# Smaller first loads in another order, and a last norm in five units, in a decoder layer on one core

## The reference, cut to what matters

```python
x = _layernorm(x + _L0_ffn_ref(x, gate_w, w1, w2, w3), axis=-1)
```

## Time and profile before

| | us |
|---|---|
| time, median of 3 runs | 710.21 |
| the three runs | 709.97, 710.21, 711.47 |
| the profiled execution, its own time | 709.6 |
| span of the profiled execution | 708.2 |
| busy in it: TensorE, VectorE, ScalarE, GpSimd | 619.1, 403.2, 236.3, 282.1 |
| mean granted TensorE clock in it | 0.925 |

### The profile page before, as it was taken

How to read it: one execution, slowest core, us unless ns; L and a number is a source line. 1 busy time by engine, 2 the same in 40 slices (tenths; PEclk the granted TensorE clock), 3 DMA queues, 4 the chain that set the end, 5 groups by cost and what they waited for, 6 DMA issues and landing times.

```text
span 708.2 us, 13714 instructions
## 1 busy us (share of the span) xinstructions
PE 619.1 (87%) x3843; PEld 495.4 (70%) x3844; DVE 403.2 (57%) x1207; ACT 236.3 (33%) x467; POOL 282.1 (40%) x195
## 2 busy tenths in 40 slices
PE   5999999798698975486999999999999999999940
PEld 2655659586366654365888888888888888888830
DVE  2566488865748769864545545545445455445524
ACT  3544550002776451223223242241422422322204
POOL 7000010011354446667513838348382274751112
PEclk9999999999899787566999999999999999999975
DMA  8999308104000033222511161512516115111116
GB/s 291 313 335 337 105 1 216 25 1 178 1 1 2 30 128 150 104 100 61 198 30 28 30 208 30 195 30 50 185 30 208 25 22 205 30 30 31 28 23 233
DMA packets 53429, 74.81 MB, mean 106 GB/s; under 512 B 13328, under 2 KB 49552, under 8 KB 52112
## 3 DMA queue, kind: packets, MB, share of 16 engines
q1 hardware_dynamic: 41056, 60.18, 25.6%
q0 software_dynamic: 6864, 9.11, 7.4%
q10 hardware_dynamic: 5472, 5.06, 2.7%
HBM read 42.67 MB, written 31.67 MB: 105 GB/s over the span
## 4 chain that ended last, share of the span: by engine, by line
PE 68%; DVE 15%; POOL 5%; ACT 5%; issue 3%; DMA 3%; POOLq 0%; ACTq 0%; DVEq 0%; SPq 0%
PE bank L2146 27%; PE bank L2166 12%; PE bank L1727 7%; PE bank L1877 4%; PE bank L2156 4%; POOL experts_w L796 3%; PE bank L1737 2%; DVE region L1230 2%; DVE region L1228 1%; DVE small L1247 1%; PE bank L2026 1%; PE bank L2132 1%; ACT region L1103 1%; PE bank L1982 1%; PE bank L2045 1%
## 5 line engine op out<-in xcount | busy, mean ns | idle before, releaser
L2146 PE MATMUL bank<-experts_w,experts_x 128*128 x864 | 218.7, 402 | 3.6 <-POOL experts_w L796 2.3
L2146 PEld LDWEIGHTS bank<-experts_w,experts_x 128*128 128x128 f32 x864 | 158.7, 190 | 37.6 <-issue 4.5
L1659 DVE TENSOR_TENSOR region<-region,bank 128x512 f32<-128x512 f32 x72 | 49.5, 688 | 165.0 <-ACT region L1054 165.0
L1054 ACT ACTIVATE region<-bank 128x512 f32<-128x512 f32 x72 | 43.0, 597 | 244.7 <-PE bank L2146 244.7
L809 POOL DMA_INDIRECT total<-region,rid x36 | 55.7, 1548 | 171.5 <-DVE region L1673 123.9
L2166 PE MATMUL bank<-experts_w 128*128 x864 | 121.1, 290 | 2.1 <-DVE experts_w L1663 2.1
L2166 PEld LDWEIGHTS bank<-experts_w 128*128 128x128 f32 x864 | 107.9, 191 | 2.5 <-issue 2.3
L796 POOL TENSOR_TENSOR experts_w<-wstage,experts_w 128x3072 f32 x12 | 83.4, 6948 | 0.5
L677 POOL TENSOR_TENSOR small<-small 128x4 f32<-128x4 f32 (+4 forms) x18 | 24.6, 1371 | 106.3 <-DVE small L1239 85.6
L1727 PE MATMUL bank<-xcol,region 128*128 128x512 f32 x128 | 57.9, 610 | 8.9 <-DMA xcol<-in_xT 7.3
L1126 DVE SCALAR_TENSOR_TENSOR region<-bank,convw,region 128x511 f32<-128x511 f32 (+2 forms) x48 | 35.9, 749 | 39.1 <-ACT region L852 37.2
(11 more groups left out here) (333 smaller groups left out, 894.3 us busy)
## 6 DMA issues: line engine op xcount, KB each, us to landing
wstage<-in_w_exp SPq DMA_DIRECT2D x8, 3072.0 KB, 10.7
slots<-padrow SPq DMA_DIRECT2D x8, 2210.0 KB, 19.8
region<-slots ACTq DMA_DIRECT2D x38, 130.0 KB, 2.1
xcol<-in_xT SPq DMA_DIRECT2D x4, 512.0 KB, 7.3
xtok<-in_x SPq DMA_DIRECT2D x1, 2048.0 KB, 12.8
region<-in_ctxT SPq DMA_DIRECT2D x1, 2048.0 KB, 7.9
region<-in_ctx SPq DMA_DIRECT2D x4, 512.0 KB, 9.0
region<-total SPq DMA_DIRECT2D x4, 512.0 KB, 5.5
```

Source lines behind the costliest of these rows:

```text
L1054: act.activation(gsil[:, u], bank[2 * u][:, :], ACT.Silu).then_inc(sil_done, 1)
L1659: dve.tensor_tensor(hmid[:, u], gsil[:, u], bank[2 * u + 1][:, :], ALU.mult).then_inc(mid_done, 1)
L2146: mm = pe.matmul(bank[2 * u + m][:, :], (xTh, xTl)[a][:, s, k, :], moving(off, w, m * KD * F + k * F + u * HALF, HALF), start=(k == 0 and ...
```

## The change

The start: `W_in` comes in four pieces, the first 128 columns of `x_proj` ahead of xT of batch 0; the taps and the bias follow with a semaphore of their own (`ld_taps`), then the first 128 columns of `z`, then the rest of either half, then `wxT`, then xT of batches 1 to 3. TensorE waits for the pieces one by one, ScalarE and VectorE for `ld_taps` in place of `ld_conv`.

The end: the four units of four tiles become five, of 2, 4, 4, 4 and 2 tiles, in the loads, the statistics, the power, the shift, the normalization and the writes.

```diff
+ENDS = ((0, 2), (2, 4), (6, 4), (10, 4), (14, 2))
...
-            sp.dma_start(winT[:, :, 0:DI], w_in[:, :, 0:DI]).then_inc(ld_win[0], 16)
+
+            def weights_of(n, first, last):
+                sp.dma_start(winT[:, :, first:last], w_in[:, :, first:last]).then_inc(ld_win[n], 16)
+            weights_of(0, 0, P)
             input_of(0)
-            sp.dma_start(winT[:, :, DI:], w_in[:, :, DI:]).then_inc(ld_win[1], 16)
-            input_of(1)
-            sp.dma_start(convw, conv_w.rearrange("(j p) k -> p j k", p=P)).then_inc(ld_conv, 16)
-            sp.dma_start(convb[:, :], conv_b).then_inc(ld_conv, 16)
+            sp.dma_start(convw, conv_w.rearrange("(j p) k -> p j k", p=P)).then_inc(ld_taps, 16)
+            sp.dma_start(convb[:, :], conv_b).then_inc(ld_taps, 16)
+            weights_of(1, DI, DI + P)
+            weights_of(2, P, DI)
+            weights_of(3, DI + P, 2 * DI)
             sp.dma_start(wxT, w_xT.rearrange("(j p) n -> p j n", p=P)).then_inc(ld_conv, 16)
-            for b in range(2, B):
+            for b in range(1, B):
                 input_of(b)
...
-            for b in range(B):
-                rsqrt(NQ, NQ * b)
+            for first, n in ENDS:
+                rsqrt(n, first)
...
-                    act.wait_ge(ld_conv, 16 * 3)
+                    act.wait_ge(ld_taps, 16 * 2)
...
-            for b in range(B):
-                act.wait_ge(shift_done, b + 1)
-                for k in range(NQ):
-                    n, row = NQ * b + k, ya[:, NQ * b + k, :]
-                    ins = act.activation(row, row, ACT.Identity, bias=shift[:, n:n + 1], scale=rsy[:, n:n + 1])
+            for u, (first, n) in enumerate(ENDS):
+                act.wait_ge(shift_done, u + 1)
+                for k in range(first, first + n):
+                    row = ya[:, k, :]
+                    ins = act.activation(row, row, ACT.Identity, bias=shift[:, k:k + 1], scale=rsy[:, k:k + 1])
                 ins.then_inc(fin_done, 1)
...
-            dve.wait_ge(ld_conv, 16 * 3)
+            dve.wait_ge(ld_taps, 16 * 2)
...
-            for b in range(B + 1):
-                if b < B:
-                    dve.wait_ge(y_back[b], 16)
-                    norm_stats(NQ * b, NQ, 1e-5, NQ * b, ya)
-                if b:
-                    n = slice(NQ * (b - 1), NQ * b)
-                    dve.wait_ge(rs_done, asked[0] - (1 if b < B else 0))
+            for u in range(len(ENDS) + 1):
+                if u < len(ENDS):
+                    first, n = ENDS[u]
+                    dve.wait_ge(y_back[u], 16)
+                    norm_stats(first, n, 1e-5, first, ya)
+                if u:
+                    first, n = ENDS[u - 1]
+                    n = slice(first, first + n)
+                    dve.wait_ge(rs_done, asked[0] - (1 if u < len(ENDS) else 0))
...
             for n in range(B * NJ):
                 if n % NJ == 0:
                     pe.wait_ge(ld_xT[n // NJ], 16)
+                if n == 1:
+                    pe.wait_ge(ld_win[2], 16)
                 project("xp", n)
-                if n == 0:
-                    pe.wait_ge(ld_win[1], 16)
+                if n < 2:
+                    pe.wait_ge(ld_win[1 + 2 * n], 16)
```

More of the change, by code:

```diff
@@ L409, in decoder_kernel @@
         drained = [sem(f"bank{k}_drained") for k in range(8)]
-        ld_conv, ld_x, ld_small, ld_ctx = (sem(f"{n}_loaded") for n in ("conv", "x", "small", "ctx"))
-        ld_win, ld_xT = [sem(f"win{n}_loaded") for n in range(2)], [sem(f"xT{b}_loaded") for b in range(B)]
+        ld_taps, ld_conv, ld_x, ld_small, ld_ctx = (sem(f"{n}_loaded") for n in ("taps", "conv", "x", "small", "ctx"))
+        ld_win, ld_xT = [sem(f"win{n}_loaded") for n in range(4)], [sem(f"xT{b}_loaded") for b in range(B)]
         consts_done = sem("consts_done")
@@ L444, in decoder_kernel @@
             "slots_cleared", "first_loaded", "first_silu_done", "first_high_done", "first_sent"))
-        y_back = [sem(f"yback{b}_loaded") for b in range(B)]
+        y_back = [sem(f"yback{n}_loaded") for n in range(len(ENDS))]
         shift_done, fin_done, out_done = sem("shift_done"), sem("fin_done"), sem("out_done")
@@ L539, in _, with rows_of @@
                 sp.wait_ge(y_sent[s], sent)
-            for b in range(B):
-                sp.dma_start(ya[:, b * NQ:(b + 1) * NQ, :], total[b * S:(b + 1) * S, :].rearrange("(i p) d -> p i d", p=P)
-                             ).then_inc(y_back[b], 16)
-            for b in range(B):
[L544 to L547, removed]
+            def rows_of(t, u):
+                first, n = ENDS[u]
+                return t[first * P:(first + n) * P, :].rearrange("(i p) d -> p i d", p=P)
+            for u, (first, n) in enumerate(ENDS):
+                sp.dma_start(ya[:, first:first + n, :], rows_of(total, u)).then_inc(y_back[u], 16)
+            for u, (first, n) in enumerate(ENDS):
+                sp.wait_ge(fin_done, u + 1)
+                sp.dma_start(rows_of(out, u), ya[:, first:first + n, :]).then_inc(out_done, 16)
+            sp.wait_ge(out_done, 16 * len(ENDS))
         def scan_step_by_step(pool):
@@ L1757, in _ @@
                         pe.wait_ge(consts_done, 1)
-                        pe.wait_ge(ld_conv, 16 * 3)
+                        pe.wait_ge(ld_conv, 16)
                     scan_inputs(n // NJ - 1)
```

## The result

The changed kernel took **708.18 us** (median of 17 runs, 703.55 to 709.77), the kernel before 710.26 us (17 runs, 705.75 to 711.52): a ratio of 0.9963 with a 95% interval of 0.9947 to 0.998. The profiled execution of the change took 708.43 us with a span of 707.0, against 709.6 and 708.2.

The account below looks back on a forecast made before the run. The prediction took TensorE's chain to bound the kernel, with waits at the start and ScalarE plus the last write at the end; -1.25 - 0.2 - 0.35 = -1.8 us gave 708.4 against a 710.21 median, range 706.9 to 710.3.

Parts of the forecast that it names:

- xT at 5.9: Start: xT of batch 0 lands at 5.9 instead of 7.16, TensorE starts at 6.05, 1.25 us earlier.
- Rival 1: Start gives nothing: xT needs its 5.56 us regardless of bytes ahead; only the end's 0.55 remains, 709.65; chance 0.14.
- The lower bound of 4.0: Start: 512 KB alone took 4.0 us, so xT, issued at 1.60, lands not before 5.6.
- the 0.4 us that the prediction worked out from the page: Start: at 138 GB/s the first 128 KB takes 0.95 us instead of some 0.55, making the sum -1.4 instead of -1.8.
- No wait for the pieces: Start: TensorE never waits for `W_in` pieces; `z` 0's 128 KB lands near 7.0, needed at 9.6, cover 2.6 us.
- ScalarE 1.25 us earlier, with its table load at 9.7: Start: taps land near 6.5 to 7, so ScalarE and its 1.28 us table load, placed after the wait, start 1.25 earlier.
- TensorE's tie with bank 0: Start: TensorE wanted the bank at 15.60 and had it within the usual 0.24; this tie moves as a whole.
- `scan_inputs` near 28.7: Start: the first `scan_inputs` comes near 28.7 in place of 29.93.
- The end, 0.55 us: After the last expert: ScalarE's end 0.2 us earlier and the smaller last write 0.35 us shorter.
- Rival 4: End gives nothing: unit 1 lands as late as 694.2 and ScalarE's gap eats the write's saving; 709.0; chance 0.12.
- The gain travels through: Between start and end: the stretch is untouched and paced by TensorE, so the start's 1.25 us gain should reach the end.
- rival 3: Clock falls elsewhere: one more half-speed fall gives 710.0 (chance 0.13), one fewer 706.8 (chance 0.08).

Follow-up runs that it names:

- the later one: The change run again beside the kernel before on one chip: 708.69 us (12 runs) against 709.83 (23 runs), ratio 1.0002.
- start alone: The change with its end set back to four units of four tiles, against the kernel before: 707.71 us against 709.68, ratio 0.9975.
- small last unit: The change with end units of 4, 4, 4, 2 and 2 tiles: one run, 704.04 us.
- VectorE last: The change with end units of 2, 4, 4, 2, 4, VectorE normalizing the last; 708.59 us against 710.89 for the kernel before, ratio 0.9973.
- early matmuls: The change plus nine constant matmuls before TensorE's first wait, against the kernel before: 702.82 us, ratio 0.9916; repeated, 706.68 us, ratio 0.9962.
- end alone: The kernel before with only the change's end, its start set back: 708.74 us, ratio 0.9984 against the kernel before.
- the one run with a pause of 2.1 us: The change with the 128 KB of weights for `z` 0 moved behind xT of batch 1 and `wxT`: one run, 713.45 us.
- the pieces alone: `W_in` in four pieces, taps and bias left behind xT of batch 1, end as before: 709.50 us, ratio 1.0006 against the kernel before.
- the taps alone: Taps and bias ahead of the second half of `W_in`, kept in two halves, end as before: 709.50 us, ratio 1.0003 against the kernel before.

## Why the prediction was right

It said 708.4 for the median and 1.8 us of gain; measured were 708.18 and 2.1. That the median came out this near is in part luck. The profiled pair differs by 1.2 us, not 1.8, since 0.6 of the start's gain was lost on the way. And the times of either kernel lie in two groups: in this comparison 6 of the 17 runs of the change are below 707 and 1 of 17 before, in the later one 2 of 12 and 8 of 23, with 1.1 us between the medians. The two local gains do not rest on the median. By its steps, in the profile of the change:

- **xT at 5.9.** It landed at 5.73, 4.13 us after its issue; in the seven profiles with 640 KB up to its end whose chain shows it it took 3.90 to 4.86 us, 4.29 in the mean, which is the forecast 5.9 (the change twice, start alone, small last unit, VectorE last, early matmuls twice). Rival 1 falls. The lower bound of 4.0 was 0.1 too high. The windows show that the smaller pieces moved more slowly: 213 GB/s up to 4.8 us where the earlier trace rows have 236. The landing came all the same 0.2 us before the time taken from bytes, so the small first piece cost nothing that could be seen. (The Trainium skill, "DMA: Bandwidth & Descriptors", section Bandwidth, gives small transfers a lower rate. The trace agrees in direction, but the taps' small pieces lie in the same stretch, and the 0.4 us that the prediction worked out from the page did not appear in the landing.)

```profile
2.00:4.80 2.80, 0.00 (x0) 0.00 (x0) 0.00 (x0) 0.00 (x0) 2.26 (x9) 1.00 0.78 213
```

- **No wait for the pieces.** None: the 128 KB for `z` 0 took 3.3 us from 3.16 and were there at 6.5 (7.0 expected), 3 us before they were needed; the 384 KB pieces at 8.0 and 9.1.
- **ScalarE 1.25 us earlier, with its table load at 9.7.** This step was wrong. The prediction had the table load behind the wait for `xp` 0; it stands behind the wait for the bias and ahead of the other. VectorE gained 2.57 us (13.12 to 10.55), not 1.25. It cost nothing in the sum, since TensorE's tie with bank 0 became a slack, and it is what let the early matmuls work later.
- **`scan_inputs` near 28.7.** 28.79, 28.59 in the second profile. The term that strayed is the number of slow matmuls, which the prediction had fixed at 3.55 us: the 48 took 22.24 to 23.84 us over the profiles without early matmuls in which TensorE met no wait of its own.
- **The end, 0.55 us.** 0.6: ScalarE's start at 6.58 (6.8 expected), gap 1.02 (0.95), end at 15.71 (15.9), last write 2.7 us (2.5). Each was within 0.25. The two terms were off in opposite directions: ScalarE's end gave 0.35 in place of 0.2, the rest up to the end of the span 0.24 in place of 0.35. GpSimd's power of two columns took 0.72 us, not the 1.01 of four. Rival 4 falls: unit 1's statistics began 4.46 us after the issue, not 5.5.
- **The gain travels through.** It did until 136 us. Then one longer stretch of half clock took 1.5, and by the loads of `total` 0.6 was left. So this step was not right as it stands: what lies between is untouched, but the clock in it moved. That is rival 3, which happened inside the very execution that was profiled, beside the forecast and not in place of it; the range, which was to take it in, begins at 706.9, 0.1 above its lower side. With the first matmul at 5.7 to 7.3 us, 3 to 7 gaps behind it were slow, and that moment does not settle how many: at 7.26 (end alone) they were 7, at 7.29 4. The statement in the Trainium skill, "TensorE: Matmul & The Clock Gate", Part 1, that the gate's interval does not start with the kernel, fits this.

The ratio's interval in the first comparison excludes no change, and in the later one it does not. With all runs of both taken together (29 of the change in two comparisons, 92 of before in four), the medians are 708.5 and 709.9, 1.4 us apart, a little under the profiles' own sum of 1.2 + 0.6. Sorted at 707 after the fact, the upper group's medians are 708.7 and 710.1, again 1.4 apart. That a single program spreads over 5 us is shown; that the change's moment of starting makes the quick patterns more or less frequent was not settled.

## What to carry to other kernels

An engine's first data should be asked for in the order of need, but two waits that end together are worth moving together: in the profiles the pieces alone gave nothing, the taps alone 0.4 us at most, both 1.2 us. While TensorE waits for its first data, let it multiply constants: nine matmuls made the next 48 run at full clock and won more than the reordering itself. And where a time of one program spreads over more than the gain, compare moments in the profiles, counted from a common event, and treat a single good time (704.04 here) as a sign of where the clock fell, not of the edit.

## What was not expected of the hardware

- The first matmuls' slow stretch is not fixed: with TensorE starting at rest, 3 (small last unit) to 7 (end alone) of the first gaps were longer than 0.6 us, 1.6 us of difference in the time of the 48. In the one run with a pause of 2.1 us right there, four more slow matmuls followed it.
- ScalarE's first table load stood between the waits of its activation: behind the DMA's, ahead of TensorE's (6.21 for an activation at 9.65; 11.35 with the taps late). Its 1.28 us left the path when the DMA came early.
- The power on GpSimd took 0.72 us for 128x2 and 1.01 for 128x4.
- The last write of 512 KB took 3.6 us with two others issued in the 1.6 us before it, and 2.9 in the kernel before, where the one ahead had been issued 2 us earlier.
